# Two images to each weight instruction in the two blurs of a four-layer convolution kernel

## What is computed

```python
def blur(x, gauss_kernel, w1, b1, w2, b2):          # x: (8, 16, 64, 64), gauss_kernel: (9, 9)
    h = relu(einsum('bchw,co->bohw', x, w1) + b1)   # 32 hidden channels
    ks = relu(einsum('bohw,o->bhw', h, w2) + b2) * 20 + 1
    sigma = ks / 3                                  # one width for each image and pixel
    wgt = exp(-gauss_kernel / (2 * sigma**2))       # 81 weights for each image and pixel
    wgt = wgt / sum(wgt over the 81)
    low = sum over the 81 offsets (u, v) of  shifted(x, u, v) * wgt[u, v]
    e = x + low
    return (e - mean(e)) / sqrt(var(e) + 1e-5)      # over the pixels of each image and channel
```

## Time and profile before

| | us |
|---|---|
| runs, median of three | 515.1 |
| the three runs | 515.1, 520.95, 514.4 |
| span of the profiled execution | 516.5 |
| PE busy in it | 431.7 (84%) |
| DVE busy | 374.6 (73%) |
| ACT busy | 279.2 (54%) |
| POOL busy | 57.2 (11%) |

### The profile page before, as it was taken

One profiled execution on the slowest core, in us unless ns is written; L12 is line 12 of the kernel. 1 busy time (PEld: TensorE's weight loads), 2 busy tenths in 40 slices (PEclk: granted clock), 3 DMA queues, 4 the chain that ended last, 5 costly groups with the idle time before them and its releaser, 6 DMA issues. The chain is left out here.

```text
span 516.5 us, 16761 instructions
## 1 busy us (share of the span) xinstructions
PE 431.7 (84%) x7248; PEld 311.4 (60%) x7248; DVE 374.6 (73%) x563; ACT 279.2 (54%) x382; POOL 57.2 (11%) x76
## 2 busy tenths in 40 slices
PE   4578998877999649689999998469978899999971
PEld 2277952224988512357777787357746687777860
DVE  2695486763888875488999999239525899999953
ACT  0655476663333200189888888211015888888753
POOL 3230002321000000310000120000030000000000
PEclk9968999997999959999999999869987999999986
DMA  8840000000000000000000000000000000000004
GB/s 189 173 171 1 2 1 0 1 0 1 3 3 1 3 0 0 0 2 4 3 4 1 0 2 4 3 1 1 0 0 1 3 4 3 3 0 1 3 4 162
DMA packets 8088, 9.79 MB, mean 19 GB/s; under 512 B 5391, under 2 KB 6752, under 8 KB 7904
## 3 DMA queue, kind: packets, MB, share of 16 engines
q1 hardware_dynamic: 7008, 8.60, 6.0%
q10 hardware_dynamic: 1024, 0.36, 0.4%
HBM read 6.85 MB, written 2.11 MB: 17 GB/s over the span
## 5 line engine op out<-in xcount | busy, mean ns | idle before, releaser
L1110 DVE TENSOR_TENSOR g_wgt<-g_exponents,ps 128x1024 f32<-128x1024 f32 x128 | 150.9, 1206 | 4.4 <-PE ps L955 4.3
L1054 ACT ACTIVATE g_wgt<-g_wgt 128x1024 f32<-128x1024 f32 x128 | 132.4, 1061 | 18.6 <-DVE g_wgt L1110 17.7
L955 PE MATMUL ps<-ident,g_scl 128*128 128x128 f32 x512 | 78.9, 283 | 4.5 <-DVE g_scl L1101 3.6
L970 PE MATMUL ps<-g_wgt,g_xt 128*32 128x64 f32 x4096 | 72.6, 223 | 7.5 <-issue 7.4
L970 PEld LDWEIGHTS ps<-g_wgt,g_xt 128*32 128x32 f32 x4096 | 62.0, 111 | 27.2 <-issue 24.1
L955 PEld LDWEIGHTS ps<-ident,g_scl 128*128 128x128 f32 x512 | 56.3, 139 | 16.0 <-DVE g_scl L1101 4.7
L1038 ACT ACTIVATE g_hid<-ps,vec 128x512 f32<-128x512 f32 x32 | 22.0, 688 | 64.5 <-PE ps L914 64.5
L469 PE MATMUL ps<-conv_img,projblk 128*32 128x512 f32 x256 | 35.4, 673 | 0.0
L1351 PE MATMUL ps<-high,wb 128*128 128x512 f32 x72 | 30.6, 426 | 5.3 <-DVE rest L1380 5.3
L526 ACT ACTIVATE biased<-ps,beta_o 128x512 f32<-128x512 f32 x32 | 23.5, 746 | 13.6 <-PE ps L469 13.5
L1061 ACT COPY g_num<-ps 128x512 f32<-128x512 f32 x32 | 18.5, 578 | 22.0 <-PE ps L970 22.0
(11 more groups left out here) (163 smaller groups left out, 688.8 us busy)
## 6 DMA issues: line engine op xcount, KB each, us to landing
x<-in_x SPq DMA_DIRECT2D x8, 256.0 KB, 6.9
x<-in_x SPq DMA_DIRECT2D x1, 2048.0 KB, 8.2
out<-g_result SPq DMA_DIRECT2D x4, 512.0 KB, 3.9
windows<-band SPq DMA_DIRECT2D x4, 256.0 KB, 4.9
c_weight<-in_c_weight SPq DMA_DIRECT2D x1, 576.0 KB, 3.8
g_w<-in_g_w SPq DMA_DIRECT2D x2, 128.0 KB, 2.6
onehot<-in_onehot ACTq DMA_DIRECT2D x1, 128.0 KB
g_gband<-in_g_gband SPq DMA_DIRECT2D x2, 64.0 KB, 2.8
```

Source lines behind the costliest of these rows:

```text
L955: tr = pe.transpose(ps[:, u % 4, P * k:P * k + P], spread(scl[s][:, k, u:u + 1], [P, P]), ident[:])
L970: mm = pe.matmul(ps[32 * j:32 * j + 32, O_BANK, 64 * cb:64 * cb + 64], xt[(s + t) % 2][:, cb, b, :], wgt[s][b][:, t, cb, :], start=(t == 0 ...
L1054: act.activation(w, w, ACT.Exp).then_inc(weight, 1)
L1110: dve.tensor_tensor(wgt[s][u][:], spread(gband[:].unsqueeze(2), shape), spread(s_in, shape), ALU.mult).then_inc(logit, 1)
```

## The change

Each product and each exponential handles two images. Images u and u+1 (u even) share a tile `wgt[s][u // 2]` of 128 x (2, 2, 8, 64), 2048 elements in a partition, with the image as the second axis. `dve_logit` reads two neighbouring PSUM banks at once and waits for both spreads; it and `act_weight` are issued at u = 0, 2, 4, 6 only. The counts of `logit` and `weight` change to pairs: `pe_spread` waits, at even u, for the product of the pair that used its two banks last; `pe_blur` waits for two exponentials for a half, not four. The number of elements, the spreads and the matmuls stay as they are.

```diff
--- before.py
+++ after.py
@@ -859,7 +859,7 @@
     sm = [sb(f"sm{i}", [P, 4 * B]) for i in range(2)]
     relu = sb("relu", [P, P])
     scl = [sb(f"scl{s}", [P, 4, B]) for s in range(2)]
-    wgt = [[sb(f"wgt{s}{u}", [P, 2, CB, BLK * BLK]) for u in range(B)] for s in range(2)]
+    wgt = [[sb(f"wgt{s}{u}", [P, 2, 2, CB, BLK * BLK]) for u in range(B // 2)] for s in range(2)]
     num = [sb(f"num{s}", [P, BANK]) for s in range(2)]
     rz = sb("rzb", [P, 4, HALF])
     mix = sb("mix", [P, 4, B, C])
@@ -949,8 +949,8 @@
 
         if u == 0:
             pe.wait_ge(small, 4 * r + 4)
-        if not (is0(r) and u < 4):
-            pe.wait_ge(logit, 8 * r + u - 3)
+        if u % 2 == 0 and not (is0(r) and u < 4):
+            pe.wait_ge(logit, 4 * r + u // 2 - 1)
         for k in range(4):
             tr = pe.transpose(ps[:, u % 4, P * k:P * k + P], spread(scl[s][:, k, u:u + 1], [P, P]),
                               ident[:])
@@ -959,7 +959,7 @@
     def pe_blur(pe, r, s, i, part):
 
         if part == 0:
-            pe.wait_ge(weight, 8 * r + 4 * i + 4)
+            pe.wait_ge(weight, 4 * r + 2 * i + 2)
             pe.wait_ge(xt_out, 2 * r + 4)
             if not (is0(r) and i == 0):
                 pe.wait_ge(num_out, 2 * r + i)
@@ -968,7 +968,7 @@
                 for j in range(HALF):
                     b = HALF * i + j
                     mm = pe.matmul(ps[32 * j:32 * j + 32, O_BANK, 64 * cb:64 * cb + 64],
-                                   xt[(s + t) % 2][:, cb, b, :], wgt[s][b][:, t, cb, :],
+                                   xt[(s + t) % 2][:, cb, b, :], wgt[s][b // 2][:, t, b % 2, cb, :],
                                    start=(t == 0), stop=(t == 1))
         if part == 1:
             mm.then_inc(blurred, 1)
@@ -1049,8 +1049,8 @@
 
     def act_weight(act, r, s, u):
 
-        act.wait_ge(logit, 8 * r + u + 1)
-        w = wgt[s][u][:].rearrange("p t k m -> p (t k m)")
+        act.wait_ge(logit, 4 * r + u // 2 + 1)
+        w = wgt[s][u // 2][:].rearrange("p t i k m -> p (t i k m)")
         act.activation(w, w, ACT.Exp).then_inc(weight, 1)
 
     def act_num(act, r, i):
@@ -1062,7 +1062,7 @@
 
     def act_row(act, r, s, do):
         for u in range(B):
-            if do.main:
+            if do.main and u % 2 == 0:
                 act_weight(act, r, s, u)
             if u < 2 and do.first:
                 act_hidden(act, 1, u)
@@ -1102,13 +1102,13 @@
 
     def dve_logit(dve, r, s, u):
 
-        dve.wait_ge(scl_spread, 8 * r + u + 1)
+        dve.wait_ge(scl_spread, 8 * r + u + 2)
         if not (isinstance(r, int) and r < 2):
             dve.wait_ge(blurred, 2 * r + u // 4 - 3)
-        shape = [P, 2, CB, BLK * BLK]
-        s_in = ps[:, u % 4, :].rearrange("p (k m) -> p k m", k=CB).unsqueeze(1)
-        dve.tensor_tensor(wgt[s][u][:], spread(gband[:].unsqueeze(2), shape), spread(s_in, shape),
-                          ALU.mult).then_inc(logit, 1)
+        shape = [P, 2, 2 * CB, BLK * BLK]
+        s_in = ps[:, u % 4:u % 4 + 2, :].rearrange("p i (k m) -> p (i k) m", k=CB).unsqueeze(1)
+        dve.tensor_tensor(wgt[s][u // 2][:].rearrange("p t i k m -> p t (i k) m"),
+                          spread(gband[:].unsqueeze(2), shape), spread(s_in, shape), ALU.mult).then_inc(logit, 1)
 
     def dve_mix(dve, r, i):
 
```

## The result

| | before | changed |
|---|---|---|
| median of four runs, us | 516.95 | 582.48 |
| lowest and highest | 514.4, 520.95 | 577.21, 590.26 |
| span of the profiled execution | 516.5 | 582.0 |

The ratio is 1.125, with a 95% interval of 1.114 to 1.135: 65.5 us slower. The forecast was a time of 582 us. One of the changed kernel's four runs (590.26) is left out of the ratio; its mean granted clock was the lowest of the four, 0.895 against 0.916 to 0.924.

A forecast was written before the change was run, and what follows sets the result against it. PE was taken to bound the kernel, and coarser hand-overs to make it wait. 515.1 us plus 51 for waits and row ends in both blurs plus 17 for the clock made 583, put at 582 for the tails; range 558 to 592.

The forecast's parts named there:

- PE's order is the bound: Steady blur rows: PE busy 66.25 of 67.24 us in five rows, so cheaper DVE and ACT work wins nothing.
- Durations: Paired product 2.26 us, paired exponential 1.95; 64 pairs save 5 us on DVE and 4 on ACT.
- (a): Relu stands behind product pair 2-3; spread 3 to PE's turn goes from 2.54 to 3.26 us, 0.72 wait a row.
- (b): ACT's copies stand behind exponential pair 4-5; spread 5 to first hidden matmul goes from 3.37 to 6.09 us a row.
- (c): Hidden layer on ACT stands behind exponential pair 6-7; ready at 8.35 us, wanted at 8.65: covered by 0.3, cost 0.
- (d): Spreads wait on the product of the pair two back, met early except for spread 0: cost 0.
- The row: A steady blur row takes 16.72 us against 13.45, +3.27, set by the loop of hand-overs.
- The clock: Falls to 1.2 GHz behind most long PE waits: 1.2 us for each of 14 rows, 17 us.
- A: Rival: not slower, the slack of DVE and ACT takes up the coarser steps; 513 to 517 us; chance 0.07.
- C: Rival: (b) comes out 1 us a row shorter and the clock holds; 552 us; chance 0.07.
- B: Rival: the waits come, but no falls of the clock; 566 us; chance 0.22.
- D: Rival: exponential pair 6-7 comes 1 us later, second hidden matmul waits 0.7 more in 12 rows; 590 to 592; chance 0.07.

The follow-up runs named there:

- all the moves: Changed kernel with ACT's copies and hidden layer, DVE's relu (except in row 0), square and reciprocal ahead of the paired instructions: 521.46 us, ratio 1.007.
- control: Kernel before, single images, with the same moves of order on ACT (copies, hidden layer) and DVE (relu, square, reciprocal): 510.54 us, ratio 0.987.
- DVE's moves: Changed kernel with relu ahead of product pair 2-3, square and reciprocal ahead of pair 4-5, ACT's order left: 589.53 us, ratio 1.139.
- the filler: Changed kernel with 16 unneeded PE transposes before the first hidden matmul of rows 0 to 5 in each blur: 571.76 us, ratio 1.104.
- copies ahead: Changed kernel with ACT's two copies of the next row's pixels ahead of the exponential of images 4 and 5: 560.86 us, ratio 1.083.

## Why the prediction was right, point by point

- *PE's order is the bound, cheaper work on DVE and ACT is worth nothing.* Right for the sign. ACT's 4.6 us less busy time bought nothing; with all the moves, pairs (521.5) stay 11 us over single images with the moves (510.5). The Trainium skill says that breaking up instructions of these two engines may help where they aren't saturated but cause bubbles on others (Perfetto Trace Analysis, Optimizing Scalar/DVE Operations). The runs agree: each engine's pairs undone alone gave 10 to 19 us back. The size of one statement was off: that a gain was limited to "1 us in five rows". A control gained 1.9 in four (0.48 a row). The step that failed took PE's busy time of 66.25 in 67.24 us as work. PE's busy time counts modelled ends, and 0.26 us a row of it went without a matmul less. The stretch was also misread: with 1713 matmuls, where four rows have 1320, it runs 1.35 us into a sixth row, and its fifth is a shorter one (12.28 us). Four steady rows have 53.61 us, 13.40 a row, and PE was already waiting 0.26 for the copies in most of them.
- *Durations.* 2.26 and 1.95 us were forecast, 2.27 and 1.91 measured. The saving was right for ACT (4 us forecast, 4.6 measured) and wrong for DVE (5 forecast, none in its busy time). Two single products in a row take 2.28 us from start to end and a pair 2.29, so a pair doesn't free DVE earlier. In four rows with all the moves, where little waits, DVE is busy 49.72 us with pairs and 49.40 with single images, ACT 42.77 and 44.26. The line for single images stands above, with the control; the line for pairs is this:

```profile
251.86:305.63 53.77, 52.53 (x1316) 41.44 (x1316) 49.72 (x57) 42.77 (x40) 9.06 (x9) 1.00 0.01 2
```

- *(a).* 3.26 forecast, 3.29 measured; taken out by DVE's moves, a row at full clock loses 0.8 us.
- *(b).* 6.09 forecast, 6.15 measured. Shown by its parts: 0.9 us a row less with ACT's exponentials single; and with the copies and the hidden layer ahead, 1.8 to 2 less.
- *(c).* Covered by 0.3 us in the forecast, no wait measured. That it is what comes next was shown by the copies going ahead alone.
- *(d)* cost nothing apart, but spread 0's wait for the pair is what remained (0.3 us) when all else was moved.
- *The row.* 16.72 forecast, 16.8 to 17.0 measured at full clock. Row 0: the first hidden matmul of row 2 moved from 11.68 us after the first spread (217.99 to 229.67) to 14.95 (217.29 to 232.24), 3.3 against 3.4. Waits and ends: 51 forecast; the kernel with the filler, which has few falls left in the blurs, is 54.0 us over the kernel before.
- *The clock.* The right cause, with a sum that was too large: I put 1.2 us on each of 14 rows, 17 in all, and the filler took 10.7 off. In the first blur two of rows 2 to 5 had falls and cost 2.1 to 2.4 us each, and a fall hit row 0. Over rows 0 to 6 of both blurs the trace has seven falls, in 14 rows: they begin at 232.2, 266.3, 286.8, 426.8, 437.0, 454.1 and 474.6 us. The price of a fall was set too low because I took the mean clock of 0.66 after two falls before as the measure: here the stretch after a fall is at 0.52 and fully on the row's path, 1.6 us between the first hidden matmul and the next spread alone. Their frequency was set too high: there are half as many falls as rows. What remains open is which of them; rows alike in their work differed in this.
- *The rivals.* A (not slower) and C (shorter waits) are out by the rows. B, the waits without falls at 566, is what the filler made of the kernel, 571.8. D is out: no wait at (c).

That 582 came out within 1 us is luck: the waits were set 3 us too low and the clock 6 us too high, and within the clock term the low price of a fall and the high number of falls cancelled in part. The kernel before also came out at 516.95 us beside it, not at the 515.1 that the sum starts from.

## What to carry to other kernels

Before you merge instructions on an engine that isn't the bound, follow the bound engine's order and ask for each wait in it: what stands, on the other engine, between the event that allows the work and the step that is waited for. Merging saved ACT 0.07 to 0.09 us a pair and DVE nothing, and put 2.8 us into one such path. Move the short steps that the bound engine waits for ahead of the long ones first, all that share a path together: one alone only shifts the wait, and in this kernel the moves without the merge were the version that won.

## What the runs showed of the hardware that I had not expected

- Idle time of PE has a second price that doesn't follow its sum. Take rows 2 to 5 of both blurs, eight rows of each kernel. Waits of about 0.6, 1.0 and 1.5 us, with 3 us of work between the last two, brought the clock down in none of them (copies ahead). Waits of 0.6, 1.0 and 1.6, with only 0.65 us of work between the last two, did in three (the changed kernel). Waits of 0.3 and 2.4 did in six (DVE's moves). A single wait of 2.3 did in all eight (single products, paired exponentials), at about 1.5 us each in the first blur. Removing 0.8 us of waiting made the kernel no faster, as it joined two gaps. This is an order and not a rule: with single exponentials the waits were 0.6, 1.0 and 0.8, less than in the kernel that never fell, and three of eight rows had a fall.
- Useless matmuls in a gap can pay: 192 transposes took 10.7 us off the changed kernel, 168 took 19 off the one with single products, 240 took 20 to 25 off the one with DVE's moves.
- A product that reads two PSUM banks at once runs at the rate of one: 2273 ns for 2048 elements against 1206 for 1024 is 1.04 ns an element.
